# A two-layer cross-attention and expert kernel: the router's order, the place of the raw weights' loads and of the waits for the projection's stores, seven banks for the first maxima, twelve spare products

## The reference, cut to what matters

```python
x = x + L0_xattn(layernorm(x), ctx, Wq, bq, Wk, bk)   # softmax(q k^T) over the context, applied to x itself
x = x + L0_ffn(layernorm(x), gate_w, gate, up, down)  # router: layernorm(x) @ gate_w.T, top 2 of 8 experts, F = 352
x = x + L1_xattn(layernorm(x), ctx, pos, pos, Wq, Wkv, Wout, bout)   # 32 heads of 16, rotary angles, softmax
x = x + L1_ffn(layernorm(x), Wg, Wu, Wd, Wr, Ag, Bg, Au, Bu, Ad, Bd) # dense part and low-rank experts
```

## Time and profile before

| | us |
|---|---|
| median of 3 runs | 1728.85 (1728.18 to 1734.74) |
| the profiled execution | 1729.65 |
| its span, first to last instruction | 1727.9 |
| TensorE busy | 1615.1 (93%) |
| VectorE busy | 1066.3 (62%) |
| ScalarE busy | 784.2 (45%) |
| GpSimd busy | 457.4 (26%) |
| mean granted clock of TensorE, of full speed | 0.965 |

### The profile page before, as it was taken

One profiled execution on the slowest core, in us unless ns is written; L12 is line 12 of the kernel. 1 busy time (PEld: TensorE's weight loads), 2 busy tenths in 40 slices (PEclk: granted clock), 3 DMA queues, 4 the chain that ended last, 5 costly groups with the idle time before them and its releaser, 6 DMA issues. The chain is left out here.

```text
span 1727.9 us, 25136 instructions
## 1 busy us (share of the span) xinstructions
PE 1615.1 (93%) x8556; PEld 1188.6 (69%) x8556; DVE 1066.3 (62%) x1959; ACT 784.2 (45%) x1239; POOL 457.4 (26%) x422
## 2 busy tenths in 40 slices
PE   6987689999959889999999989989999999999998
PEld 5776679999947653433343347668888888888886
DVE  5886733222248877898888837655555547545456
ACT  5653223332334526878877763453333332223232
POOL 1210023332237751111110001332322223233232
PEclk8998789999988978999999999999999999999999
DMA  8996126663255764222232211443333246422221
GB/s 271 340 359 227 55 80 228 233 223 138 74 183 173 241 182 107 76 67 65 75 75 62 70 20 49 151 166 125 103 115 126 84 160 256 164 68 76 87 68 49
DMA packets 110364, 236.40 MB, mean 137 GB/s; under 512 B 39888, under 2 KB 53840, under 8 KB 101536
## 3 DMA queue, kind: packets, MB, share of 16 engines
q1 hardware_dynamic: 104000, 214.33, 37.1%
q0 software_dynamic: 6240, 20.45, 3.5%
HBM read 274.84 MB, written 93.45 MB: 213 GB/s over the span
## 5 line engine op out<-in xcount | busy, mean ns | idle before, releaser
L1319 DVE TENSOR_REDUCE early_top<-r_ring 128x1 f32<-128x512 f32 x480 | 304.2, 680 | 33.6 <-PE r_ring L1330 29.3
L2045 ACT ACTIVATE r_probs<-r_st 128x1024 f32<-128x1024 f32 x256 | 248.0, 1021 | 42.7 <-PE r_st L1958 39.9
L48 PE MATMUL f_bank<-late_xnT,late_weights 128*128 128x512 f32 x1056 | 252.4, 392 | 0.0
L48 PEld LDWEIGHTS f_bank<-late_xnT,late_weights 128*128 128x128 f32 x1056 | 196.8, 188 | 40.9 <-issue 0.7
L2835 DVE TENSOR_TENSOR attn<-attn,f_bank 128x512 f32<-128x512 f32 x132 | 90.7, 687 | 195.0 <-PE f_bank L48 130.7
L48 PE MATMUL m_bank<-w_place,m_xT 128*128 x936 | 168.1, 329 | 3.0 <-DVE m_xT L1220 3.0
L2829 ACT ACTIVATE attn<-f_bank 128x512 f32<-128x512 f32 x132 | 78.9, 598 | 180.0 <-PE f_bank L56 125.5
L48 PEld LDWEIGHTS m_bank<-w_place,m_xT 128*128 128x128 f32 x936 | 153.5, 191 | 6.9 <-issue 3.6
L1330 PE MATMUL r_ring<-early_slots 48*128 48x512 f32 x352 | 141.1, 475 | 4.9 <-PEq L1372 1.3
L1330 PEld LDWEIGHTS r_ring<-early_slots 48*128 48x128 f32 x352 | 58.6, 186 | 118.7 <-DVE early_top L1319 109.4
L1987 PE MATMUL r_out<-r_probs,early_v 128*17 128x512 f32 x1024 | 136.5, 605 | 0.5 <-ACT r_probs L2045 0.3
(11 more groups left out here) (330 smaller groups left out, 2788.5 us busy)
## 6 DMA issues: line engine op xcount, KB each, us to landing
w_place<-expert_split SPq DMA_DIRECT2D x72, 1408.0 KB
w_place<-expert_split SPq DMA_DIRECT2D x36, 1024.0 KB
late_w_dram<-late_weights SPq DMA_DIRECT2D x11, 1920.0 KB, 8.1
expert_split<-w_place SPq DMA_DIRECT2D x10, 1408.0 KB
w_place<-expert_split SPq DMA_DIRECT2D x36, 384.0 KB
late_weights<-late_w_dram SPq DMA_DIRECT2D x11, 1024.0 KB, 5.1
late_weights<-late_w_dram SPq DMA_DIRECT2D x11, 896.0 KB, 4.8
early_slots<-y_rows SPq DMA_DIRECT2D x16, 512.0 KB, 7.3
```

The source lines that it names most:

```text
L48: last = nc.tensor.matmul(out, l, r, start=(i == 0), stop=(i == len(passes) - 1))
L1319: return nc.vector.reduce_max(self.top[g % 2][:, q, h:h + 1], bank[:], AXIS_X)
L2045: nc.scalar.activation(probs[k][:, 2 * pair:2 * pair + 2, :], st_ps[pair][:], ACT.Exp, scale=SCALE).then_inc(exp_done, 1)
```

## The change

1. **Norms early.** The `TokenNorm` object is made outside both phases. In the last batch of the first attention VectorE aggregates tiles 0 to 11 in three lots of four, ScalarE takes the root, and VectorE the reciprocal as its last work. The last four tiles follow inside the router loop.
2. **Router three ahead.** VectorE normalises three tiles ahead of its subtraction; TensorE's product follows its turn by two tiles instead of one; the split tile has three places instead of two (the third in the space of `hT`); the gate weights are turned after the second tile, in a bank of their own. The constants' memsets come after the loop.
3. **Raw weights later.** SyncE issues the last expert's five loads ahead of the store of tile 10.
4. **Waits in the attention.** `qk_out` belongs to `AttentionInputs`; the projection's last wait is taken out. GpSimd waits for all pairs ahead of its loop; SyncE waits for 15 pairs ahead of the load in group 0 and for all 16 in group 16.
5. **Seven banks.** From product 16 on the maxima go round seven banks. The order is: maxima up to 16, the turn of the shift, maxima 17 to 31.
6. **Twelve spare products**, in the shift's bank, once that has been copied.

```diff
+def token_moments(nc, n, tiles):
+    for t in tiles:
         nc.vector.bn_aggr(n.moments[:, t, :], n.stats[:, t, :])
+def token_var(nc, n, tiles):
     nc.vector.drain()
+    nc.vector.tensor_scalar_add(n.var[:, tiles], n.moments[:, tiles, 1], EPS).then_inc(n.var_ready, 1)
+EARLY_TILES, LATE_TILES = slice(0, TILES - TPB), slice(TILES - TPB, TILES)
...
@@ phase_attention0, ScalarE and VectorE
                 for t in range(TPB):
                     prep(b, 3 + t)
+                    if not ahead and t == TPB - 2:
+                        token_std(nc, act, norm, EARLY_TILES, 1)
...
                 for t in range(1, TPB):
+                    if not ahead:
+                        token_moments(nc, norm, range((t - 1) * TPB, t * TPB))
+                        if t == TPB - 1:
+                            token_var(nc, norm, EARLY_TILES)
                     add(b, t)
                     final_stats(b, t - 1)
                     prep(b, 3 + t)
                 final_stats(b, TPB - 1)
+            token_rstd(nc, dve, norm, EARLY_TILES, 1)
...
@@ phase_moe0, SyncE
-            for unit in range(3 * (E0 - 1), weights.UNITS):
-                weights.load(sp, unit)
             for i in range(TILES):
                 sp.wait_ge(n.xn_ready, i + 1)
+                if i == TILES - XN:
+                    for unit in range(3 * (E0 - 1), weights.UNITS):
+                        weights.load(sp, unit)
+                sp.wait_ge(n.xn_ready, i + 1)
                 sp.dma_start(xn_rows[i * P:(i + 1) * P, :], rows[:, i % XN, :]).then_inc(xn_out[i % XN], DMA)
...
@@ phase_moe0, TensorE
-            pe.wait_ge(gw_in, DMA)
-            turn(x_banks[0], [gw_raw[:, k * P:(k + 1) * P] for k in range(DK)], x_turned)
             for i in range(TILES):
                 pe.wait_ge(n.xn_ready, i + 1)
-                wait_count(pe, x_split, i)
-                turn(x_banks[(i + 1) % 2], [rows[:, i % XN, k * P:(k + 1) * P] for k in range(DK)], x_turned)
-                if i:
-                    router(i - 1)
-                if i % TPB == 1 and i > TPB:
+                wait_count(pe, x_split, i - 1)
+                turn(x_banks[i % 2], [rows[:, i % XN, k * P:(k + 1) * P] for k in range(DK)], x_turned)
+                if i == 1:
+                    pe.wait_ge(gw_in, DMA)
+                    turn(gw_bank, [gw_raw[:, k * P:(k + 1) * P] for k in range(DK)], gw_turned)
+                if i >= 2:
+                    router(i - 2)
+                if i % TPB == TPB - 1 and i > TPB:
                     turn_logits(i // TPB - 1)
+            router(TILES - 2)
             router(TILES - 1)
...
@@ phase_moe0, VectorE
+            for i in range(3):
+                normed_rows(i)
+            for i in range(TILES):
+                lo_x(i)
+                if i == 0:
+                    dve.wait_ge(gw_hi, 1)
+                    nc.vector.tensor_tensor(gwT[:, LO].rearrange("p k e -> p (k e)"), gw_bank[:, 0:DK * E0],
+                                            fp32(gwT[:, HI].rearrange("p k e -> p (k e)")), ALU.subtract).then_inc(gw_split, 1)
+                if i == 2:
+                    token_moments(nc, n, range(TILES - TPB, TILES))
+                    token_var(nc, n, LATE_TILES)
+                if i == TPB + 2:
+                    token_rstd(nc, dve, n, LATE_TILES, 2)
+                if i + 3 < TILES:
+                    normed_rows(i + 3)
...
@@ phase_qkv1
+    def pairs_stored(self, engine, pairs):
+        for i, out in enumerate(self.qk_out):
+            engine.wait_ge(out, self.QK_STORES * DMA * len(range(i, pairs, self.QK_RING)))
...
+        wide_ps = (qk_ps[0][1], *qk_ps[1], *v_ps, *xt_ps)
+        def max_bank(n):
+            return max_ps[n % 4] if n < HEAD_TILES else wide_ps[(n - HEAD_TILES) % 7]
...
             store_pair(pair_of(B - 1, 3))
-            for i in range(RING):
-                sp.wait_ge(qk_out[i], STORES * DMA * len(range(i, PAIRS, RING)))
...
+                    elif n < HEAD_TILES:
+                        pe.wait_ge(max_read, n - 3)
+                    elif n < HEAD_TILES + 3:
+                        pe.wait_ge(roped, (pair_of(B - 1, 2), pair_of(B - 1, 3), pair_of(B - 1, 3))[n - HEAD_TILES] + 1)
                     else:
-                        pe.wait_ge(max_read, n - 3)
-                    early.maximum(nc, g, g, q, h, max_ps[n % 4]).then_inc(max_ready, 1)
+                        pe.wait_ge(max_read, n - 6)
+                    early.maximum(nc, g, g, q, h, max_bank(n)).then_inc(max_ready, 1)
...
-            first_maxima(12, 8)
+            first_maxima(12, 5)
             turn_first_shift()
-            first_maxima(20, 12)
-            spare_products(nc, 8, qk_ps[0][1], wv[:, HI, 0, 0:P], wv[:, HI, 1, :])
+            first_maxima(17, 15)
+            pe.wait_ge(shift_copied, 1)
+            spare_products(nc, 12, shift_ps, wv[:, HI, 0, 0:P], wv[:, HI, 1, :])
...
@@ phase_rope_attention1, GpSimd and SyncE
+            early.pairs_stored(pool, B * 4)
             for g in range(GROUPS):
...
                     wait_count(sp, out_ready, g)
+                    if g == 0:
+                        early.pairs_stored(sp, B * 4 - 1)
+                    if g == GROUPS // 2:
+                        early.pairs_stored(sp, B * 4)
                     early.load(sp, scr, g + RING - 1, (g + RING - 1) % RING)
```

More of the change, by code:

```diff
@@ L84, in tile_stats, with token_rstd, token_std @@
                        x[:, ds(tile, 1), :].rearrange("p t d -> p (t d)"))
-def token_var(nc, n):
-    for t in range(TILES):
+def token_moments(nc, n, tiles):
+    for t in tiles:
         nc.vector.bn_aggr(n.moments[:, t, :], n.stats[:, t, :])
+def token_var(nc, n, tiles):
     nc.vector.drain()
-    nc.vector.tensor_scalar_add(n.var[:], n.moments[:, :, 1], EPS).then_inc(n.var_ready, 1)
-def token_rstd(nc, dve, n):
-    dve.wait_ge(n.std_ready, 1)
-    nc.vector.reciprocal(n.rstd[:], n.std[:])
+    nc.vector.tensor_scalar_add(n.var[:, tiles], n.moments[:, tiles, 1], EPS).then_inc(n.var_ready, 1)
+def token_rstd(nc, dve, n, tiles, round_):
+    dve.wait_ge(n.std_ready, round_)
+    nc.vector.reciprocal(n.rstd[:, tiles], n.std[:, tiles])
     nc.vector.drain()
-def token_std(nc, act, n):
-    act.wait_ge(n.var_ready, 1)
-    nc.scalar.activation(n.std[:], n.var[:], ACT.Sqrt).then_inc(n.std_ready, 1)
+def token_std(nc, act, n, tiles, round_):
+    act.wait_ge(n.var_ready, round_)
+    nc.scalar.activation(n.std[:, tiles], n.var[:, tiles], ACT.Sqrt).then_inc(n.std_ready, 1)
 def normalise_tile(nc, n, x, tile, out):
@@ L286, with phase_attention0 @@
 PREP_ATTENTION = PREP_FIRST + B * PREP_BATCH
[L289 removed]
+def phase_attention0(nc, io, x, ident, stats, weights, norm):
     from contextlib import ExitStack
@@ L1085, in _, with lo_x, normed_rows @@
         def _(dve):
+            def lo_x(i):
+                dve.wait_ge(x_hi, i + 1)
+                nc.vector.tensor_tensor(xr[i % 3][:, LO], x_banks[i % 2][:].rearrange("p (k c) -> p k c", k=DK),
+                                        fp32(xr[i % 3][:, HI]), ALU.subtract).then_inc(x_split, 1)
+            def normed_rows(i):
+                if i >= XN:
+                    dve.wait_ge(xn_out[i % XN], DMA * (i // XN))
+                    dve.wait_ge(x_turned, i - XN + 1)
+                normalise_tile(nc, n, x, i, rows[:, i % XN, :])
+            for i in range(3):
+                normed_rows(i)
+            for i in range(TILES):
+                lo_x(i)
+                if i == 0:
+                    dve.wait_ge(gw_hi, 1)
[8 more added lines that the diff above has]
+                    normed_rows(i + 3)
             for i in range(E0):
@@ L1091, in _ @@
                 nc.vector.memset(a[:, 0:E0], 0.0)
-            token_var(nc, n)
-            token_rstd(nc, dve, n)
-            def lo_x(i):
-                dve.wait_ge(x_hi, i + 2)
-                nc.vector.tensor_tensor(xT[:, i % 2, LO], x_banks[(i + 1) % 2][:].rearrange("p (k c) -> p k c", k=DK),
-                                        fp32(xT[:, i % 2, HI]), ALU.subtract).then_inc(x_split, 1)
-            for i in range(TILES):
-                if i >= XN:
-                    dve.wait_ge(xn_out[i % XN], DMA * (i // XN))
-                    dve.wait_ge(x_turned, i - XN + 2)
-                normalise_tile(nc, n, x, i, rows[:, i % XN, :])
-                if i == 0:
-                    dve.wait_ge(x_hi, 1)
-                    nc.vector.tensor_tensor(gwT[:, LO].rearrange("p k e -> p (k e)"), x_banks[0][:, 0:DK * E0],
-                                            fp32(gwT[:, HI].rearrange("p k e -> p (k e)")), ALU.subtract).then_inc(x_split, 1)
-                else:
-                    lo_x(i - 1)
-            lo_x(TILES - 1)
             dve.wait_ge(consts, 5)
@@ L1310, in __init__ @@
         self.ones_set = ctx.enter_context(nc.semaphore("early_ones_set"))
+        self.qk_out = [ctx.enter_context(nc.semaphore(f"early_qk_out{i}")) for i in range(self.QK_RING)]
+    def pairs_stored(self, engine, pairs):
```

(7 more changed lines are left out.)

43 lines of the change are left out of this document (25 added, 18 removed).

## The result

The changed kernel takes 1719.16 us (median of 5 runs, 1717.95 to 1720.24); the kernel before took 1728.85 beside it (5 runs, 1724.5 to 1734.74). The ratio is 0.9941, interval 0.9917 to 0.9964. A later session repeats it with more runs of the kernel before (experiment 12): 0.9956, 0.9942 to 0.9970, which is 7.6 us of 1727.2. The forecast was 1722.0. The profiled executions are 1729.65 and 1717.95, 11.7 apart, so not all of that distance is the change's.

The account below looks back on a forecast made before the run. It took one chain of waits to set the end at each place: the router's product wait and SyncE's store wait at the boundary. Gains 4.5 + 2.05 + 0.3 = 6.85 us gave 1722.0, range 1718 to 1726.5.

Parts of the forecast that it names:

- signs of being wrong: Router tiles still 1.4 apart, TensorE awaiting a transfer near 182, barrier still following a DMA, or first group under 12.5 us.
- rival A: Second attention's start: it begins at full clock and keeps it; gain 9.1 us in all, 1719.7; chance 0.15.
- Router: start and pace, 4.5: Router: earlier first product and 1.16 us a tile bring the last product 4.5 us earlier; bounds 3.0 to 5.6.
- Rival B: Router: its pace stays and only the start gains; 3.85 us in all, 1725.0; chance 0.1.
- Raw weights later, 0: Expert stage: five loads moved behind earlier stores land in time, cost 0; removing them from the head gains nothing.
- Boundary, 2.05: Projection's end: SyncE's store wait goes, VectorE is late next, attention starts 2.05 us earlier; bounds 0.9 to 2.4.
- rival C: Projection's end: spare products at half clock hold the barrier; gain 0.8 instead of 2.05, 1723.2; chance 0.08.
- The hiccup of 0.3: Projection's end: VectorE's second maxima read waits for a matmul behind the last rotation; 0.1 to 0.5 us, taken as 0.3.
- The attention's own waits, 0: Second attention: the waits put there ask for stores already landed; cost 0, or 0.5 us if uncovered.
- Clock of the first group, 0.3: Attention's first group: the clock falls again after the spare products; 0.3 us gained, between 1.5 lost and 2.6 gained.
- D: Projection's end: the moved wait does nothing, as SyncE awaits its transfers anyway; gain 4.5 + 0.3, 1724.0; chance 0.07.
- E: Expert stage: raw weights land late, slower beyond 18 us of landing; 1737.7 at 27 us; chance 0.03.

Follow-up runs that it names:

- experiment 12: The changed kernel run again, unedited, for its scatter: 1720.0 us, ratio 0.9956 against the kernel before.
- experiment 6: The changed kernel with eight spare products instead of twelve: 1722.0 us, ratio 0.9975 against the kernel before.
- experiment 9: The changed kernel with TensorE's router product one tile behind its turn, as before: 1721.68 us, ratio 0.9970 against the kernel before.
- experiment 10: The changed kernel with the first twelve tiles' norms back in the expert stage: 1720.73 us, ratio 0.9959 against the kernel before.
- experiment 7: The changed kernel with the last expert's raw weights loaded at the head of the expert stage again: 1724.68 us, ratio 0.9990 against the kernel before.
- experiment 11: The kernel before with only the raw weights' loads moved behind the tenth tile: 1726.95 us, ratio 1.0001 against the kernel before.
- experiment 1: The changed kernel with the projection's end and the attention as before, leaving the router's parts: 1723.99 us, ratio 0.9982 against the kernel before.
- experiment 3: The changed kernel with SyncE's wait for all stores put back at the projection's end: 1718.89 us, ratio 0.9955 against the kernel before.
- experiment 5: The changed kernel with four banks and the old order of the maxima, keeping twelve spare products: 1722.97 us, ratio 0.9981 against the kernel before.
- experiment 8: The changed kernel with another order of the seven banks: 1719.03 us, ratio 0.9959 against the kernel before.
- experiment 2: The kernel before with only the seven banks, twelve spare products and moved waits: 1722.73 us, ratio 0.9976 against the kernel before.
- experiment 4: The changed kernel without any spare products: 1723.38 us, ratio 0.9981 against the kernel before.

## Why the prediction was right, and where it was not

The time fell inside the range and 2.8 us under the forecast, but the account behind it holds in the router's size and in the waits of the attention, and fails at the boundary and in the clock. One of the prediction's own signs of being wrong came true, a first group under 12.5 us (11.23), and VectorE is not the last engine before the barrier. The time is nearer to rival A's 1719.7, which had a chance of 0.15, than to the forecast's 1722.0; it stayed in the range because that took in A's time. Step by step:

**Router: start and pace, 4.5.** Right: 4.45. From the last statistics to the first product I had 6.1 (156.8 to 162.9), it took 5.70; to the last product 25.3, it took 25.37. The pace came out at 1.16 a tile and 0.34 for a turn of the logits, with no hiccup, but the clock rose some 2 us later than I took it: at 164.5, 9.4 behind the last statistics, instead of 7.4. The first product 0.4 early and the missing hiccup of 0.3 pay for the late clock, some 0.8: that the sum came out within 0.1 is luck. With the clock up 6.7 behind the statistics the same router took 23.92 (experiment 6), a gain of 5.9 and beyond my upper bound of 5.6. Experiments 9 and 10 divide the gain: the products' longer distance 2.9, the norms 1.1. They and the loads are not terms that add: 2.9, 1.1 and 2.4 (experiment 7) are each what the new router loses without one of them, and together more than it gains. Rival B, in which the pace stays, is out. That the early norms cost nothing in the first attention held too: its last batch took 28.5 to 28.6 us with and without them, wherever the clock was alike.

**Raw weights later, 0.** Half wrong. That moving them costs nothing held (6.6 us of landing, no wait). "Removing them from the head gains nothing either, because nothing there waited for a transfer" failed. It was true of the kernel before (experiment 11) and false of the changed one: I read the absence of a wait in the old profile and did not ask what the quicker router would reach. It normalises further ahead and sooner comes to the seventh tile, which needs the first row buffer again, while the first stores are still behind 2.1 MB. 2.4 us of the router's 4.45 hang on this edit.

**Boundary, 2.05.** Measured 1.50, and some 1.0 against the two other traces with the old boundary (13.25 and 13.19, experiments 1 and 11). Two things in the step failed. First, the engine that is late next is TensorE, not VectorE: the attention follows the spare products by 0.3 and VectorE by 1.0. That is rival C's place, but not its price, since the clock did rise. Second, the maxima "without a gap, 0.44 each" did not happen. The two products of a pair lie in different halves of the rows and overlap: two of them take 0.42 to 0.59 us even at half clock, so TensorE was level with VectorE after 2 us and then walked in its steps of 0.6, as before. The spare products nevertheless began at 7.2 behind the rotation, close to my 6.7 + 0.6, and the clock rose in them (3.6 us after their start). I had the right time for a wrong reason. The wait's removal, which I took for the whole of the term, is worth 0.3 beside twelve spare products (experiment 3); what makes room is the seven banks (2.2, experiment 5). The 0.3 is small also because SyncE's last stores begin 0.8 to 1.1 earlier there than in the traces with the old boundary. With stores as late as in those they would land 12.7 to 13.2 behind the last rotation, and the wait would be worth some 1.0 to 1.5 (an estimate: that landing plus the 0.5 from it to the attention, less 12.2); experiment 8 has such late stores, no wait, and a boundary of 12.00. The hiccup of 0.3 was there and is hidden (experiment 8). A wait that goes is worth the distance to the next engine, not its own length.

**The attention's own waits, 0.** Right: nothing waits there for a store between 640 and 700.

**Clock of the first group, 0.3.** This is the mis-sized term: 2.7. "After the change the spare products end some 1.7 us before the phase does, so I expect the fall again". They ended 0.26 before the phase, since TensorE was itself the last, and the level did not fall; rival A's 2.6 came. The rule of the Trainium skill that I weighed (TensorE: Matmul & The Clock Gate, "HAM oscillation — how this bites in real kernels"), that idle stretches between bursts bring the low clock back, is not refuted: where the clock had risen and TensorE then idled 1.3 or 1.2 us (experiment 11), it fell within the first group; behind a pause of 0.3 to 0.6 the first group kept the full clock in nine traces (after and experiments 2, 3, 6, 7, 8, 9, 10 and 12). In experiments 1 and 4 it had not risen before the attention, so they say nothing of the fall. The step that failed was the length of the pause, which I took from VectorE's end: 1.7 us forecast, 0.3 measured. That the short pause is what kept the clock is argued from these traces and not shown, since no run has twelve spare products, or seven banks with a risen clock, ahead of a long pause; experiment 3 was meant to be that run, and its pause was 0.57. Eight products before VectorE has finished caught the full clock in the one execution of experiment 6 that has a trace, and by the scatter of its times not in all, while twelve caught it in each that has a trace, but for experiment 5, where it came just behind the attention's start.

**Sum.** Router 4.45, boundary 1.0 to 1.5, first group 2.7: 8.2 to 8.7, against 7.6 timed, interval 5.2 to 10.0. The rest of the 11.7 between the profiles lies ahead of the router, between the two places and behind the attention's first group, where traces whose edits should not matter there differ as much. Rivals D and E are out: D's gain of the boundary did come, though hardly from the wait, and E's landing was 6.6 and not beyond 18.

No variant beat the change. Fewer spare products gain 0.7 at the barrier and risk 3.4 in the first group (experiment 4); another order of the banks and the wait put back are worth nothing that can be measured.

## What to carry to other kernels

When a wait at a barrier is removed, price the distance to the engine that arrives next, and include the filler that keeps the clock up: work added only to hold the clock can itself become the last arrival, and that is good as long as the time it saves by the clock (here 3.4 us) exceeds the delay it makes (0.7). An edit that is worth nothing alone can be what another edit stands on: look up which resource the faster loop will run out of (here six row buffers behind one queue), not only which one the old loop waited for. And before two profiles are compared, cut both at landmarks, and ask of each stretch how much it differs between traces in which nothing there was changed; here the first and the last, 2.7 of 11.7 us, lay within that.

## What the runs showed of the hardware

- Products of 48 rows in different halves of the rows follow one another, in pairs, at 0.42 to 0.59 us for two, so 0.21 to 0.3 each, at the granted clock 0.50, where products over all 128 rows (the spare ones) start 0.44 apart. The Trainium skill (TensorE: Matmul & The Clock Gate, "Part 3: Packing small matmuls — row/col tiling") says that small matmuls in distinct row groups run concurrently; the trace agrees.
- The barrier itself is short: 0.35 us from VectorE's end to the next phase when nothing else is late (experiment 4), 0.26 to 0.3 from TensorE's modelled end (after).
- Stores of 256 KB behind 2.1 MB of loads in one queue landed in 8.1 us, without the loads ahead of them in 2.0.
- One DMA issue of SyncE took 1.40 to 1.85 us among neighbours of 0.6 in five traces (before, experiments 1, 5, 8 and 11), at one of pair 14's stores or the load behind them, and in none of the other nine. The last pair's stores then began 0.7 to 1.2 us later. The cause is open.
